# One memset per rest, range loads inside the runs, later score steps, and two of five groups of expert rows weighed by ScalarE and added by POOL

## What is computed

```python
edge_index = jnp.stack([src, dst])
xn = _layernorm(x)
x = x + gnn(xn, edge_index) + linear_attention(xn)
x = x + moe(_layernorm(x), own random edges)      # the expert stage below
xn = _layernorm(x)
x = x + gnn2(xn, edge_index) + attention2(xn)
x = x + moe2(_layernorm(x))

def moe(x, edges):                  # 4 experts, the best 2 per node
    h = (x @ W_gat).reshape(M, 4, 4)
    e = leaky_relu(a_src[src] + a_dst[dst], 0.2)   # per edge and head
    alpha = softmax of e over the edges of each dst
    agg = segment_sum(h[src] * alpha, dst)         # 16 numbers per node
    scores = layernorm(agg + b).reshape(M, 4, 4).mean(1)
    g = softmax over the top 2 scores, 0 for the others
    return sum(g[:, ei] * (gelu(x @ W1[ei] + b1[ei]) @ W2[ei] + b2[ei]) for ei in range(4))
```

## Time and profile before

| | |
|---|---|
| median of 3 runs | 4437.22 us (4434.75 to 4440.62) |
| profiled execution | 4442.14 us, its span 4440.2 us |
| granted TensorE clock, mean | 0.905 of full speed |
| PE busy | 3688.1 us (83%) |
| DVE busy | 2239.0 us (50%) |
| ACT busy | 1345.7 us (30%) |
| POOL busy | 720.6 us (16%) |

### The profile page before, as it was taken

The page is one execution under the profiler, slowest core; times in us unless marked ns, Lnnn a source line. Parts: engine busy times, 40 slices in busy tenths (PEclk is TensorE's granted clock), DMA queues, the critical chain, the costliest instruction groups (busy, mean ns, idle before and its releaser), DMA issues. The chain is left out here.

```text
span 4440.2 us, 92119 instructions
## 1 busy us (share of the span) xinstructions
PE 3688.1 (83%) x23892; PEld 2662.1 (60%) x23943; DVE 2239.0 (50%) x5781; ACT 1345.7 (30%) x2980; POOL 720.6 (16%) x1416
## 2 busy tenths in 40 slices
PE   4888867499969898996889627689798999799998
PEld 2444435366648757964777415479698544467766
DVE  6888877888840021125677330610402867533333
ACT  2555541477740010042111212410000144133333
POOL 3222210000000000001566632000001565000000
PEclk9999985688879989998999858889999999799999
DMA  3111230132234403501221211245154000100000
GB/s 110 44 71 75 84 120 0 57 95 85 66 111 160 151 5 146 202 22 18 76 63 32 40 45 57 91 148 190 62 186 166 1 1 1 21 14 14 7 14 29
DMA packets 124636, 319.63 MB, mean 72 GB/s; under 512 B 42658, under 2 KB 74897, under 8 KB 109228
## 3 DMA queue, kind: packets, MB, share of 16 engines
q1 hardware_dynamic: 111332, 302.42, 19.6%
q0 software_dynamic: 9760, 8.89, 1.4%
q10 hardware_dynamic: 3404, 6.53, 0.4%
HBM read 245.52 MB, written 72.43 MB: 72 GB/s over the span
## 5 line engine op out<-in xcount | busy, mean ns | idle before, releaser
L557 PE MATMUL ps<-hot_key,hot_src 128*126 128x512 bf16 (+1 forms) x2208 | 416.8, 314 | 38.5 <-DVE hot_key L522 21.0
L522 DVE TENSOR_SCALAR hot_key<-col_iota,run_keys 128x625 bf16<-128x625 int16 x1104 | 394.9, 380 | 0.0
L1338 PE MATMUL ps<-gnn_u_thirds,near 125*128 125x256 bf16 x3000 | 337.2, 275 | 23.3 <-issue 23.3
L557 PEld LDWEIGHTS ps<-hot_key,hot_src 128*126 128x126 bf16 x2208 | 212.5, 136 | 234.3 <-DVE hot_key L522 171.6
L1338 PEld LDWEIGHTS ps<-gnn_u_thirds,near 125*128 125x128 bf16 x3000 | 331.0, 141 | 27.8 <-issue 25.0
L2456 PE MATMUL ps<-xnT,ew 128*128 (+2 forms) x640 | 189.2, 449 | 158.3 <-ACT ehT L2564 123.7
L519 DVE TENSOR_SCALAR hot_src<-col_iota,run_srcs 128x125 bf16<-128x125 int16 x828 | 212.3, 256 | 97.0 <-PE ps L557 52.0
L2456 PEld LDWEIGHTS ps<-xnT,ew 128*128 128x128 f32 x640 | 123.1, 199 | 211.6 <-ACT ehT L2564 135.4
L866 PE MATMUL ps<-row_hot,slot_hot 128*128 128x512 f16 x1088 | 221.4, 357 | 2.3 <-DVE row_hot L1079 2.2
L3650 DVE SCALAR_TENSOR_TENSOR xres<-ps,shares,xres 125x256 f32 x200 | 96.8, 484 | 241.6 <-PE ps L3615 220.7
L2470 PE MATMUL ps<-ew,ehT 128*125 128x256 f32 x800 | 203.5, 398 | 0.0
(11 more groups left out here) (571 smaller groups left out, 6898.6 us busy)
## 6 DMA issues: line engine op xcount, KB each, us to landing
near<-adjacency SPq DMA_DIRECT2D x80, 1562.5 KB, 6.5
adjacency<-counts SPq DMA_DIRECT2D x125, 312.5 KB, 2.2
own_in<-own_rows SPq DMA_DIRECT2D x34, 512.0 KB, 4.1
expert_rows<-rows_y SPq DMA_DIRECT2D x75, 125.0 KB
rows_room<-expert_rows SPq DMA_DIRECT2D x25, 375.0 KB
pair_in<-high_rows SPq DMA_DIRECT2D x34, 256.0 KB, 4.8
pair_in<-low_rows SPq DMA_DIRECT2D x34, 256.0 KB, 5.7
rows_room<-key_rows SPq DMA_DIRECT2D x8, 1024.0 KB
```

What stands on the lines that cost most here:

```text
L522: nc.vector.tensor_scalar(hot_key[:, j, :], col_iota[:], run_keys[:, ds(at, 1), j:j + 1].rearrange("p a j -> p (a j)"), None, ALU.is_equal ...
L557: last = nc.tensor.matmul(sums[:, b:e], hot_src[:, j, :], hot_key[:, j, b:e], start=False, stop=True, skip_group_check=True)
L1338: last = nc.tensor.matmul(ps[:, j, 0:width], lead_tiles[BUF[j]][:, k, :], parts.thirds[:, k, i, :], start=(k == 0 and i == 0), stop=(k == ...
```

## The change

Four edits, in two blocks:

- Counting: TensorE loads the range of the first group of a tile at the tile's start, and that of each further group behind the first chunk of every run of the group before it. ScalarE uses the loaded start of the next group as the end of this one and so loads once per group in place of twice.
- POOL's rest has one memset, not two.
- The Exp of the last block stands in group 4 of expert 2, the root of the variance in group 3 of expert 3, the Exp of the gates inside the same group ahead of its fourth row tile, and the turning of the gates in group 4 of expert 3.
- Of the rows of experts 0 to 2, VectorE weighs and adds groups 0 to 2. Those of groups 3 and 4 are multiplied by their gate in place by ScalarE, behind its last row of expert 3, and added to `xres` by POOL, which waits for itself after each five additions. VectorE waits for POOL before it goes on to group 3 of expert 3's rows.

```diff
@@ counting, TensorE
                     with pe.Fori(0, T) as tile:
+                        _, runs, before, _ = ranges_of(mybir.EngineType.PE, tile * TG)
                         for k in range(TG):
                             group = tile * TG + k
-                            _, runs, before, _ = ranges_of(mybir.EngineType.PE, group)
...
                                     last.then_inc(hot_used, 1)
+                                    if j == 0 and k < TG - 1:
+                                        _, next_runs, next_before, _ = ranges_of(mybir.EngineType.PE, group + 1)
+                            runs, before = next_runs, next_before
@@ counting, ScalarE
-                            make_sources(tile * TG + k + 1)
-                            _, _, _, upto = ranges_of(mybir.EngineType.Activation, tile * TG + k)
-                            take_out(tile, k, upto)
...
+                            take_out(tile, k, make_sources(tile * TG + k + 1))
@@ experts, VectorE
-                        for g in range(G):
+                        dve.sem_inc(gates_kept, 1)
+                        for g in range(POOL_ROWS):
                             dve.wait_ge(rows_landed[g], 16 * TG)
...
                         for g in range(G):
+                            if g == POOL_ROWS:
+                                dve.wait_ge(pool_rows, (G - POOL_ROWS) * (EXPERTS0 - 1))
@@ experts, POOL
                                 if j % 2:
-                                    rest(b * (SLOTS // 2) + (j // 2 - SLOTS))
...
+                                    nc.gpsimd.memset(idle[:], 0.0).then_inc(rested, 1)
+                                    alone(pool, rested, b * (SLOTS // 2) + (j // 2 + 1 - SLOTS))
...
                         pool.wait_ge(ends_got, 16 * OWN)
+                        for g in range(POOL_ROWS, G):
+                            for e in range(EXPERTS0 - 1):
+                                n = (g - POOL_ROWS) * (EXPERTS0 - 1) + e
+                                for j in range(TG):
+                                    t = g * TG + j
+                                    pool.wait_ge(rows_weighed, n * TG + j + 1)
+                                    ins = nc.gpsimd.tensor_tensor(xres[:, t, :], rows_in[:, t, e, :], xres[:, t, :], ALU.add)
+                                ins.then_inc(pool_rows, 1)
+                                pool.wait_ge(pool_rows, n + 1)
@@ experts, TensorE
-                        expert(3, 1, 0, 3)
-                        expert(3, 1, 3, 4, ahead_of_rows=turn_gates)
-                        expert(3, 1, 4, G)
+                        expert(3, 1, 0, 4)
+                        expert(3, 1, 4, G, ahead_of_rows=turn_gates)
@@ experts, ScalarE
-                        expert(2, 0, 1)
-                        expert(2, 1, 2, after_piece=weigh_within(earlier * 2 + 1))
-                        expert(2, 2, G)
+                        expert(2, 0, 4)
+                        expert(2, 4, G, after_piece=weigh_within(earlier * 2 + 1))
...
-                        expert(3, 0, 2)
-                        expert(3, 2, 3, after_row=root_of_variance)
-                        act.wait_ge(marks_ready, 1)
-                        nc.scalar.activation(odds, odds, ACT.Exp).then_inc(odds_ready, 1)
-                        expert(3, 3, G)
+                        expert(3, 0, 3)
+                        expert(3, 3, 4, after_row=gate_steps)
+                        expert(3, 4, G)
+                        act.wait_ge(gates_kept, 1)
+                        for g in range(POOL_ROWS, G):
+                            act.wait_ge(rows_landed[g], 16 * TG)
+                            for e in range(EXPERTS0 - 1):
+                                for t in range(g * TG, (g + 1) * TG):
+                                    nc.scalar.activation(rows_in[:, t, e, :], rows_in[:, t, e, :], ACT.Identity,
+                                                         scale=gates[:, t, e:e + 1]).then_inc(rows_weighed, 1)
```

26 lines of the change are left out of this document (14 added, 12 removed).

## The result

| | kernel before | changed kernel |
|---|---|---|
| median of 4 runs each, us | 4438.9 (4434.8 to 4442.5) | 4341.7 (4338.2 to 4343.5) |
| span of the profiled execution, us | 4440.2 | 4341.7 |
| mean granted clock of TensorE | 0.905 | 0.911 |

The ratio is 0.978, 95% interval 0.9768 to 0.9793: 97 us less, where 131 were forecast (4306; 4342 lies within the range, which ended at 4350). The spans differ by 98.5 us.

A forecast was written before the change was run, and what follows sets the result against it. Changed stages bound by VectorE/TensorE hand-overs at group boundaries (counting) and POOL's row gather, then TensorE (experts). Counting -38 and experts -93.5 give -131.5 from 4442.1: 4310.6, or 4306 us on the median's scale; range 4280 to 4350.

The forecast's parts named there:

- one memset: POOL's row gather, expert stage: dropping the second memset saves 0.27 us in each of 128 rests, 34.6 us.
- TensorE, from resuming to its end: Expert stage: later score steps cut TensorE's time after its long stall from 209.9 to 127 us.
- from there to the last statistics: Expert stage: about 43 us from TensorE's last expert matmul to the last batch statistics, where it was 18.6.
- (a): Rival, counting stage: range loads inside the runs are on the path, so counting gains nothing; 4344 us, chance 0.13.
- (b): Rival, expert stage: SP's large row loads starve the sums gather, delaying the root, +36 us; 4342 us, chance 0.09.
- (c): Rival, POOL's row gather: a pair keeps its 3.5 us with one memset, +34.6 us; 4341 us, chance 0.06.
- ScalarE's root: Sign in expert 3: ScalarE's root of the variance sits between 2655 and 2660 on the new time scale.
- 100 x 0.38: Counting stage: at 100 group boundaries the range load leaves the gap, 0.38 us each, 38 us saved.
- The waits that should vanish: Expert stage: three ScalarE waits labelled remote, taken as waits for stores of expert 2's rows, go; 23.8 us.
- rival (e): With one memset, SP's stores starve under the whole row gather, +169 us, slower than before; 4475 us, chance 0.04.
- Late gates and the split: Expert stage: gates come at 2716.6; VectorE and POOL take turns, ending at 2770; the split alone is +3 us.
- Rival (d): Expert stage's weighing: VectorE and POOL take no turns; 4292 us, chance 0.06.

The follow-up runs named there:

- rest_in_sums_gather: The changed kernel with one memset rest after every second of POOL's 25 gathers of sums; 4319.8 us, ratio 0.9731 to the kernel before.
- later_steps_alone: The kernel before with only TensorE's and ScalarE's new order in experts 2 and 3; 4374.5 us, against 4413.9 for the kernel before in its comparison.
- two_memsets: The changed kernel with two memsets per POOL rest again; 4365.8 us, ratio 0.9833 to the kernel before.

## Why the prediction was right, and where not

The sum by its steps, expected and found (spans, us):

| step | forecast | found | missing |
|---|---|---|---|
| counting stage | -38 | -24.7 | +13.3 |
| one memset (start of stage to last scores) | -34.6 | -30.9 | +3.7 |
| TensorE, from resuming to its end | 127 | 147.0 | +20.0 |
| from there to the last statistics | 43 | 39.1 | -3.9 |
| stage between the two (not touched) | 0 | +6.4 | +6.4 |
| behind the expert stage (not touched) | 0 | -7.0 | -7.0 |

-131.5 + 32.5 = -99; the spans say -98.5. The measured 4342 is beyond the 4285 to 4330 that the forecast's own terms gave. It lies in the range only because this was carried up to 4350 for rivals (a), (b) and (c); two of them are out, and the first had a share of the miss, so that part is luck. ScalarE's root stood at 2701.8 in place of 2655 to 2660; the first three misses of the table and the one between the stages add up to 43 of these us.

**The range loads.** That the load leaves the boundary was right ('s gap falls as told). The step that failed is the term 100 x 0.38, which put the loads inside the runs at nothing. Read at the full clock, the boundaries gave some 45 us, the upper bound and not 38, and the loads inside took back some 19: "TensorE waits for VectorE there anyway" covers most of the load in groups of two runs (0.10 lost), and next to nothing in the 18 groups of one run (0.39), where the sign of the whole turns. Rival (a) had this mechanism, with twice its price. That a tile's last group lost 0.14 as well, 3 us in all, is not explained.

**The memset.** Right; 30.9 and 30.5 in two pairs of profiles for 34.6. From first to last the 256 gathers take 449.9 us in place of 482.4, 0.26 a pair for the 0.27, and the first of them comes 1.1 later in its stage; the rest is not followed further.

**The waits that should vanish.** This is the step that failed in kind: "the three waits put down to a remote are ScalarE waiting for stores of expert 2's rows, so they go", 23.8 us. In the new order ScalarE stores nothing there and crawls all the same. rest_in_sums_gather gives the cause as far as it can be shown: take away POOL's unbroken row of 25 gathers, and the crawl is gone, and with it 21.6 of TensorE's 147.0 us; 125.4 and, in later_steps_alone, 126.1 stand against the 127 of the sum, so its other terms are right together. Not each by itself: the 23.8 adds up whole waits, though ScalarE is idle 1.8 us before any copy, and TensorE's own stall under that crawl was 19.23. I had taken the label "remote" for a store because stores were near. The label says only that the profile doesn't know; that all three waits lay within the 32 us of gathers without a rest, which rival (e) itself noted, should have been weighed as a cause. Rival (e) came nearest, with gathers without rests as its condition; but it expected the same of gathers with one memset, where one rest in two is enough, and put it down to the stores.

**Late gates and the split.** Right: gates 10.9 us ahead of TensorE's end (10.4 expected), and turns between VectorE and POOL, 39.1 us for 43. By the Trainium skill, SBUF — State Buffer, section "SBUF: two separate sides", a VectorE operation with two SBUF inputs and a GpSimd operation that reads SBUF exclude each other; the 0.84 us a weighing beside POOL's additions agree in kind. By the same section of the Trainium skill the one that comes second waits for the whole instruction of the first; here a pair took 0.86 us, less than both one behind the other (0.42 + 0.67). Rival (d) is out. The price of it was read right too: the split is worth nothing.

**Rival (b)**, SP's row loads starving the sums gather: out. VectorE waited 41.29 us for the sums in place of the earlier trace rows's 39.16, with the loads beside them, and had them 47 us before the root. **Rival (c)**: out, by two_memsets.

**The untouched stages.** The stretch between counting and experts took 1453.5 to 1463.7 us in fourteen profiles of kernels that are alike there. The changed kernel's was the longest, at a granted clock of 0.829, the lowest of the fourteen; the two of 1454.0 and 1454.2 had 0.839, the highest. Its +6.4 is such scatter and not the change's. The stages behind the experts took 1568.0 to 1576.7 in the same fourteen profiles, so their -7.0 lies within the scatter as well.

## What to carry to other kernels

Before you count a wait as removed, name who releases it by an experiment or by its place in time: a label such as "remote" isn't a releaser. A work step moved into another engine's waiting time may be covered in one kind of place and not in another; sort the places by kind, take the step out and double it, and look at the granted clock before reading the difference. And where helpers share a path with the engine they relieve, look first whether its own work can start earlier: the split brought nothing, the gates a group earlier with VectorE weighing all some 20 us.

## What the runs showed of the hardware

- POOL issuing indirect DMAs without a rest can hold up ScalarE and VectorE: up to 9.2 us from one ScalarE copy to the next beside 25 gathers 1.30 us apart in the changed kernel (2.17 otherwise), and single waits up to 165 us beside 256 of them. One memset with a wait after every second gather prevented it in all profiles with such rests; one after every eighth only in part. It came in two comparisons and the first result and stayed out in a later comparison with the same gathers; transfers, packets and issue times look alike in both, so what decides is open. TensorE's semaphore updates are on record up to 19 us late in it. What a rest costs where the crawl stays out wasn't run.
- A register load on TensorE's queue took 333 ns for four values from the first of four, 535 ns for two from the second, and 1797 ns for twenty. Whether the starting place or the number makes the two slower than the four wasn't tried.
- Longer or more loads on TensorE's queue in the counting went with a lower granted clock: 0.99 in its mean with one load of 333 ns in a run, 0.97 with two, 0.95 with one of 535 ns, 0.94 with 1797 ns at each tile's start.
- Beside POOL's additions VectorE's two-input operation went from 0.42 to 0.84 us, start to start, and one of POOL's from 0.67 to 0.90 us in length.
